# An xattn + LoRA-MoE kernel on one core: the normalised rows handed to the transposes in blocks of 32 rows, by sixteen transfers in two halves instead of four

## The reference

```python
def _xattn(h, mem, mask):                     # mem: 64 rows per batch
    scores = einsum('bsd,bmd->bsm', h, mem) / sqrt(D)
    attn = softmax(where(mask, scores, -1e30))
    return einsum('bsm,bmd->bsd', attn, mem)

def _ffn(x, weight, lora_A, lora_B, router_w):
    base = einsum('btd,od->bto', x, weight)
    probs = softmax(einsum('btd,ed->bte', x, router_w))
    w_dense = top-2 of 8 experts, renormalised
    Ax = einsum('nd,erd->ner', x, lora_A)
    return base + einsum('ner,ne,eor->no', Ax, w_dense, lora_B) * 2.0

x = x + _xattn(_layernorm(x), ctx_2048, mask)
x = x + _ffn(_layernorm(x), weight, lora_A, lora_B, router_w)
```

## Time and profile before

| what | value |
|---|---|
| median of 3 runs | 999.71 us (997.89 to 1001.46) |
| the profiled execution's own time | 1000.15 us |
| its span in the trace | 998.2 us |
| PE busy | 979.6 us (98%) |
| DVE busy | 868.6 us (87%) |
| ACT busy | 476.0 us (48%) |
| POOL busy | 144.0 us (14%) |
| granted TensorE clock | full in every slice |
| four transfers `xq<-xn`, per tile | 128 KB each, median 3.5 us from issue to landing |

### The profile page before, as it was taken

How to read it: one execution, slowest core, us unless ns; L and a number is a source line. 1 busy time by engine, 2 the same in 40 slices (tenths; PEclk the granted TensorE clock), 3 DMA queues, 4 the chain that set the end, 5 groups by cost and what they waited for, 6 DMA issues and landing times.

```text
span 998.2 us, 18389 instructions
## 1 busy us (share of the span) xinstructions
PE 979.6 (98%) x5849; PEld 950.2 (95%) x5849; DVE 868.6 (87%) x2230; ACT 476.0 (48%) x930; POOL 144.0 (14%) x278
## 2 busy tenths in 40 slices
PE   8999999999999999999999999999999999999998
PEld 7899999999999999999999999999999999999998
DVE  6988988889988899889989899888999889988874
ACT  7755544545444455445455445444454444454420
POOL 3311111111111111111111111111111111111100
PEclk9999999999999999999999999999999999999999
DMA  8555565555566555664555755556565566554432
GB/s 318 180 176 149 150 173 158 160 133 158 165 162 181 148 138 152 172 189 143 138 143 160 208 138 162 130 149 193 158 159 154 128 182 171 156 156 128 112 77 70
DMA packets 156095, 156.61 MB, mean 157 GB/s; under 512 B 93968, under 2 KB 128912, under 8 KB 156048
## 3 DMA queue, kind: packets, MB, share of 16 engines
q1 hardware_dynamic: 155184, 154.63, 56.2%
q10 hardware_dynamic: 864, 1.45, 0.4%
HBM read 78.74 MB, written 33.55 MB: 112 GB/s over the span
## 4 chain that ended last, share of the span: by engine, by line
PE 36%; DVE 22%; DMA 13%; SPq 10%; issue 8%; ACT 5%; POOL 5%; ACTq 0%; POOLq 0%; DVEq 0%
PE base_ps L1107 10%; PE base_ps L1109 10%; PE base_ps L1108 10%; DMA xq<-xn 10%; SPq L381 7%; DVE stats L903 5%; ACT xn L609 4%; DVE x2T L919 4%; DVE w_raw L897 3%; POOL rstd L494 3%; PE s_ps L1134 3%; SPq L417 2%; DMA w_raw<-w_raw 2%; DVE x_first L897 2%; PE ro_ps L1179 1%
## 5 line engine op out<-in xcount | busy, mean ns | idle before, releaser
L1107 PE MATMUL base_ps<-w_hi,xT_hi 128*128 128x392 f32 x1512 | 495.5, 328 | 0.0
L1109 PE MATMUL base_ps<-w_hi,xT_lo 128*128 128x392 f32 x1512 | 494.4, 327 | 0.0
L1108 PE MATMUL base_ps<-w_lo,xT_hi 128*128 128x392 f32 x1512 | 494.4, 327 | 0.0
L1107 PEld LDWEIGHTS base_ps<-w_hi,xT_hi 128*128 128x128 f32 x1512 | 285.9, 189 | 1.7
L1108 PEld LDWEIGHTS base_ps<-w_lo,xT_hi 128*128 128x128 f32 x1512 | 285.8, 189 | 1.6
L1109 PEld LDWEIGHTS base_ps<-w_hi,xT_lo 128*128 128x128 f32 x1512 | 285.8, 189 | 0.0
L919 DVE STREAM_TRANSPOSE x2T<-xq 128x512 f32<-128x512 f32 x122 | 167.2, 1465 | 27.7 <-DMA xq<-xn 27.6
L494 POOL TENSOR_TENSOR rstd<-var_eps,neg_half 128x1 f32<-128x1 f32 x64 | 61.4, 959 | 521.8 <-DVE var_eps L910 521.8
L615 ACT CAST xT_hi<-x2T 128x512 fp32r<-128x512 f32 x122 | 69.5, 616 | 100.9 <-DVE x2T L919 100.9
L590 ACT CAST eT<-w_raw 128x128 fp32r<-128x128 f32 x59 | 17.6, 298 | 166.6 <-DMA w_raw<-w_raw 166.5
L926 DVE TENSOR_TENSOR xT_lo<-x2T,xT_hi 128x512 fp32r<-128x512 f32 x122 | 78.2, 683 | 0.0
(11 more groups left out here) (131 smaller groups left out, 1274.2 us busy)
## 6 DMA issues: line engine op xcount, KB each, us to landing
xT_raw<-in_xT SPq DMA_DIRECT2D x62, 512.0 KB, 5.2
xq<-xn SPq DMA_DIRECT2D x244, 128.0 KB, 3.5
w_raw<-in_x SPq DMA_DIRECT2D x32, 512.0 KB, 3.4
out<-x_first SPq DMA_DIRECT2D x32, 512.0 KB, 2.7
out<-w_raw SPq DMA_DIRECT2D x31, 512.0 KB, 2.8
x_first<-in_x SPq DMA_DIRECT2D x30, 512.0 KB, 3.5
h<-w_raw SPq DMA_DIRECT2D x248, 16.0 KB, 2.1
w_raw<-w_raw SPq DMA_DIRECT2D x236, 16.0 KB, 2.6
```

The lines of the kernel that those rows point to most:

```text
L1107: pe.matmul(out_, a_hi, w_h, start=start, stop=False, skip_group_check=again)
L1108: pe.matmul(out_, a_hi, w_l, start=False, stop=False, skip_group_check=again)
L1109: return pe.matmul(out_, a_lo, w_h, start=False, stop=stop, skip_group_check=again)
```

## The change

`exchange` issues sixteen transfers of 32 KB where it issued four of 128 KB. For each block g of 32 rows and each quarter a of the columns, 32 rows of 256 numbers go to place g of the 32 partitions of `xq` that belong to quarter a. So row 32g+n stands at partition n, place g, and a transpose of place g writes 32 neighbouring columns (`(g n)` in place of `(n g)`). The two transposes of a tile have a semaphore each: the first waits for the eight transfers of places 0 and 1, which are issued first, the second for the other eight. The bytes are the same.

```diff
-        xq_loaded = sem("xq_loaded")
+        xq_loaded = [sem(f"xq_loaded{i}") for i in range(TS)]
@@
                 sp.wait_ge(xn_done, count(tile, 1, 1))
-                for a in range(Q):
-                    sp.dma_start(xq[a * QP:(a + 1) * QP, :, :],
-                                 xn[:, a * DQ:(a + 1) * DQ]).then_inc(xq_loaded, 16)
+                for g in range(Q):
+                    for a in range(Q):
+                        sp.dma_start(xq[a * QP:(a + 1) * QP, g, :],
+                                     xn[g * QP:(g + 1) * QP, a * DQ:(a + 1) * DQ]).then_inc(xq_loaded[g // QS], 16)
@@
-                dve.wait_ge(xq_loaded, count(tile, 16 * Q, -16 * Q * 2))
+                dve.wait_ge(xq_loaded[i], count(tile, 16 * Q * QS, -16 * Q * QS * 2))
                 if exists(after(tile, 2)):
                     dve.wait_ge(ln1_step, count(after(tile, 2), 2, 2))
-                out_ = x2T[:, :, :].rearrange("p c (n g) -> p g c n", g=Q)
+                out_ = x2T[:, :, :].rearrange("p c (g n) -> p g c n", g=Q)
```

## The result

The changed kernel takes **1413.08 us** (median of 4 runs, 1411.59 to 1413.69) against 999.33 us before (4 runs, 997.89 to 1001.46): ratio 1.4136, 95% interval 1.4112 to 1.4160. The direction was right, the size was not: 1158 us was forecast, and the time lies above the range's upper end of 1385 us. The rival "the issue costs what it costs within the core" had given 1383.

The account below looks back on a forecast made before the run. PE's work bound the kernel at 15.14 us per tile; with sixteen issues the loop would, at 10.98 + 6.72 = 17.70 us. 60 periods of 2.56 us more, plus 4.1 us, on 1000.15 us gave 1158 us, range 1105 to 1385 us.

Parts of the forecast that it names:

- the issue costs what it costs within the core: Rival on SP's exchange issues: 0.65 us each, 21.4 us per tile, 1383 us; chance 0.30, with what lies between 0.5 and 0.65.
- the loop: Once per tile from `exchange` through softmax weights, readout, statistics, `hT_low`, `rstd` and `xn` back to `exchange`: 13.57 us before.
- The wait of SP for `xn`: SP waits 3.8 us per step; claimed to be no room for issues, since `xn` depends on work behind them.
- d = 0.42 us: Time from one exchange issue on SP to the next, ends 0.37 to 0.65; sixteen issues take 6.72 us.
- The equal shape: Reason taken for cheap issues on SP: same shape on both sides, so 0.37 to 0.45 us instead of 0.65.
- The rest of the loop, 10.98 us: The loop per tile without the exchange's issues: 13.57 us less the 2.59 us of four issues.
- a readout at half speed: Remark on PE's clock with issues of 0.65 us: pause over 6 us, under 0.7 us added to a period.
- The clock rival: PE's clock falls from 2.4 to 1.2 GHz in pauses: up to 30 us per tile and 1900 us; chance 0.03.
- pauses of 2.5 us: PE idle per tile ahead of the readout, waiting for the softmax weights; the granted clock was expected to stay full.
- The transposes: Two per tile on DVE, 730 ns each instead of 1465, saving 1.47 us per tile, hidden once the loop bounds.
- The first rival: Issue length on SP goes with its pieces: 0.16 us each, loop stays under PE, 991 us; no-loss chance 0.04.
- The halves: Separate semaphores for the two transposes' eight transfers each: cost nothing and win nothing.

Follow-up runs that it names:

- e1: The kernel before with each of the exchange's four transfers cut into four, sixteen issues per tile, old row order, transposes and single semaphore kept: 1500.15 us.
- e9: The changed kernel with its sixteen transfers reading the same shapes from an input in the outer memory instead of `xn`: 1227.59 us.
- e7: The changed kernel with the exchanges of the softmax weights and of `h`, eight issues per tile, made by ACT instead of SP: 1230.29 us.
- e2: The kernel before with each of the exchange's four transfers cut into two, eight issues per tile, nothing else changed: 1113.0 us.
- e10: The kernel before with four extra transfers per tile within the core, issued on SP behind the load of x, outside the loop: 1041.29 us.
- e5: The kernel before with groups of extra transfers on SP behind its last store; mostly 0.62 to 0.66 us each within the core, 0.44 to 0.46 from outside.
- e6: The changed kernel with idle matmuls of a constant (24 or 15) on PE ahead of each readout, filling its pauses: 1428.38 us.
- e3: The kernel before, four transfers kept, with only the transposes writing runs of 32 (columns in another order, run for time): 991.87 us.
- e11: The kernel before plus DVE transposes behind its end, writing 4, 2, 1 elements apart: 1.10, 0.74, 0.74 us at rest, 1.43, 0.82, 0.74 beside PE.
- e8: The kernel before with the exchanges of the softmax weights and of `h`, eight issues per tile, made by ACT instead of SP: 1140.05 us.

## Why the prediction was wrong, and where it was right

**What bounds the kernel, and the loop: right.** The wait of SP for `xn` was no slack, and from the changed kernel to e1 and to e9 the period moved with the issues (rests of 11.75, 11.77 and 11.45 us). e7 cuts the loop at the exchanges behind the sixteen, and 183 us come back. That is shown, not argued. Two things the prediction lacked. It took the loop from one step without the scores of two tiles; e2 shows that the steps that have them are 0.8 us longer with eight issues, through PE and DVE. And SP's waits hold less slack than their mean says, even outside the loop (e10).

**The length of an issue, d = 0.42 us: wrong, and nearly all of the miss.** The changed kernel's sixteen issues take 10.16 us where 6.72 stood in the sum: 3.44 us, over 61 exchanges 210 of the 255 us between forecast and result. The failed step is the choice between two reasons that, as the text said itself, the trace did not separate. The equal shape was taken as the reason and the place (within the core) as the lesser one; e5 shows that the place is all of it, and e9 that with issues of the outside kind the kernel would have taken 1227.6 us. The row that was nearest in kind was there: the transfers within the core take 0.6 us, at 16 and at 128 KB. It should have been the value taken, and 0.42 the bound.

**The rest of the loop, 10.98 us: too short by 0.77 us, 46 us in all.** With the issues' 210 this closes the difference of 255. Station by station against the layout of before: from `eT` to the start of the readout's sum 1.68 us (733.48 to 735.16) where 1.05 had been possible, and the sum itself 1.57 us to the statistics where it had been 1.43, since its second half now waits for PE. Both come from the readout at half speed: on the mean over the steps the same two stretches, from `eT` to the statistics, take 3.20 us, and e6 gets 0.44 us of it back with a readout that is faster. The prediction had this as a remark ("a readout at half speed would add under 0.7 us to a period") and priced it, but left it out of the range: the high end of 1385 us was the dear issues with a full clock. That is why the result fell outside even though the case that came true was among the rivals. The two rivals should have been added, since the one brings the other: the longer the issues, the longer PE's pause.

**The clock rival's test was the wrong row.** The earlier trace rows show a full clock at 3.94 of 5.00 us busy, but the longest pause in that stretch is 0.88 us (6.95 to 7.83 in PE's timeline). The pause to be judged was one of 2.5 us, and the changed kernel's is one of 6 us (727.8 to 733.8), with a clock of 0.50 behind it. In e2 a pause of 2.4 us (from 509.2, the end of the matmuls, to 511.61) was followed by a clock of 0.50 and 0.63 us matmuls as well, so the forecast's own case of pauses of 2.5 us was not safe either. The prediction had named such a clock as a sign of being wrong. The Trainium skill ("TensorE: Matmul & The Clock Gate", Part 1: The HAM clock gate) has the clock go back to half when PE idles and return after sustained work; that agrees.

**The transposes: right.** 0.73 us were forecast, 0.71 measured, hidden behind the readout as told, and worth 8.6 us where they are not hidden (e3). The first rival had 991 us for that case, and 991.87 were measured with the four transfers; that it fits so well is luck, since the rival took half of PE's 18.6 idle us "at a guess".

**The halves: right.** The second semaphore neither cost nor won: e1 with one semaphore has the same rest (11.77 against 11.75 us).

## What to carry to other kernels

Before you cut a transfer into more pieces, multiply the pieces by the issue's length in the row of the same place (here 0.6 us within the core, from 16 to 128 KB), and ask whether the wait of the issuing engine depends on work that stands behind those issues: if it does, every issue is paid in full, once per turn of the loop. A loop lengthened by one term may also open pauses for the fastest engine, so the slower clock belongs in the same case as the longer term, not in a rival of its own. And a mean wait is no slack: look at the shortest wait of the steps, and at what has just been issued ahead of it. Price a layout's gain alone first (here one line, 8.6 us), and then what each way of getting it costs.

## What the runs showed of the hardware that I had not expected

An issue on SP costs by place: 0.62 to 0.66 us from start to start within the core and 0.44 to 0.46 us from the outer memory, with 16, 32 or 128 rows alike within the core and 32 or 128 from outside (e5; in e9 0.47). Cut into pieces over eight destination rows it rose to 0.71 us (e1).

A DVE transpose that writes four elements (16 bytes) apart takes 1.10 us at rest and 1.43 us beside a running PE, one that writes two apart 0.74 and 0.82, and one with neighbouring elements 0.74 in both (e11). The Trainium skill ("SBUF — State Buffer", Door 1: The DMA port swizzle) says that full bandwidth needs two or more accesses in a row to the same 16-byte line; two elements apart still makes two to a line and was free at rest, four apart makes one and was not. That agrees; that PE at work widens the gap is from the rows alone. In the kernels it shows too: the old transposes took 1067 ns on the median in e1, where they fall into PE's pauses, and 1488 ns before.

The softmax weights' transfers of 16 KB issued from ACT in e8 landed in 3.9 us on the median where those from SP before took 2.6 (those of `h` 2.0 against 2.1), with the 512 KB loads of SP now in flight beside them; how much of it is that was not separated.
